# One-core attention and mixture-of-experts block: ring of 16 token tiles, weight copies two tiles ahead, last scatters in a row, loops written out

## What is computed

```python
x = x + _layernorm(_L0_attn_ref(_layernorm(x), ...))    # 16 heads of 8, relative bias, causal; MLP 128-512-128
x = x + _layernorm(_L0_ffn_ref(_layernorm(x), ...))

# _L0_ffn_ref, per token t:
probs = softmax(x @ router_w.T)            # 8 experts
top_w, top_idx = top_k(probs, 2)
h = silu(x @ gate_w[e].T) * (x @ up_w[e].T)    # 128 -> 352
y = sum over the two experts of top_w * (h @ down_w[e].T)   # 352 -> 128
```

## Time and profile before

| | us |
|---|---|
| median of 3 runs | 609.92 (609.04 to 613.66) |
| profiled execution, its own time | 612.49 |
| its span | 610.7 |

### The profile page before, as it was taken

How to read it: one execution, slowest core, us unless ns; L and a number is a source line. 1 busy time by engine, 2 the same in 40 slices (tenths; PEclk the granted TensorE clock), 3 DMA queues, 4 the chain that set the end, 5 groups by cost and what they waited for, 6 DMA issues and landing times.

```text
span 610.7 us, 13818 instructions
## 1 busy us (share of the span) xinstructions
PE 532.2 (87%) x4568; PEld 386.2 (63%) x4569; DVE 382.8 (63%) x1083; ACT 396.6 (65%) x873; POOL 329.4 (54%) x337
## 2 busy tenths in 40 slices
PE   6876899989889899799899897899778979999992
PEld 5552355656466456465556564798678879999940
DVE  6627465783994974999947767363766434555344
ACT  3357898879779788878897786355353434554415
POOL 4012535536618888438877357176437754454426
PEclk9757799999999999999999999599999999999997
DMA  8755331223214323213734612022112332222074
GB/s 199 111 140 115 110 99 57 78 76 103 67 41 126 102 68 115 77 36 123 178 109 148 145 51 49 11 60 64 37 44 66 89 89 62 59 62 61 18 275 137
DMA packets 48285, 55.85 MB, mean 91 GB/s; under 512 B 7868, under 2 KB 42559, under 8 KB 46064
## 3 DMA queue, kind: packets, MB, share of 16 engines
q1 hardware_dynamic: 43872, 46.59, 28.3%
q0 software_dynamic: 4352, 8.47, 4.2%
HBM read 37.19 MB, written 18.36 MB: 91 GB/s over the span
## 4 chain that ended last, share of the span: by engine, by line
PE 49%; DVE 23%; POOL 11%; ACT 7%; issue 7%; DMA 3%; DVEq 1%; ACTq 0%; POOLq 0%; SPq 0%
PE SC L806 13%; PE OA L816 6%; PE OA L683 5%; PE M L757 4%; PE M L721 4%; POOL slots L1591 3%; DVE SS L1218 2%; POOL RZ L1577 2%; PE SC L665 2%; DVE arena L406 2%; DVE A L1477 2%; ACT arena L927 2%; DVE STP L1287 1%; PE SC L669 1%; PE M L649 1%
## 5 line engine op out<-in xcount | busy, mean ns | idle before, releaser
L927 ACT ACTIVATE arena<-SC 128x1024 f32<-128x1024 f32 x160 | 163.0, 1033 | 20.8 <-PE SC L670 12.3
L806 PE MATMUL SC<-arena 128*128 128x128 f32 (+1 forms) x864 | 110.8, 279 | 10.9 <-DVE arena L1385 10.9
L1597 POOL DMA_INDIRECT ytok<-YSA,XGA x72 | 74.8, 1038 | 80.4 <-ACT YSA L1030 71.5
L806 PEld LDWEIGHTS SC<-arena 128*128 128x128 f32 (+1 forms) x864 | 102.5, 186 | 14.0 <-DVE arena L1385 12.8
L683 PE MATMUL OA<-arena 128*32 128x256 f32 (+1 forms) x1536 | 91.4, 357 | 10.0 <-DVE arena L1251 6.1
L1591 POOL DMA_INDIRECT slots<-XBA,IDX x64 | 74.4, 1162 | 47.6 <-DVE IDX L1336 31.1
L1024 ACT ACTIVATE arena<-SC 128x256 f32<-128x256 f32 (+1 forms) x144 | 39.2, 324 | 78.2 <-PE SC L806 78.1
L1379 DVE TENSOR_TENSOR arena<-arena,SC 128x256 f32<-128x256 f32 (+1 forms) x144 | 44.2, 348 | 70.0 <-ACT arena L1024 70.0
L683 PEld LDWEIGHTS OA<-arena 128*32 128x32 f32 x1536 | 39.4, 110 | 49.6 <-issue 19.8
L406 POOL TENSOR_TENSOR arena<-arena 128x512 f32<-128x512 f32 x32 | 41.5, 1298 | 53.8 <-ACT arena L927 53.4
L816 PE MATMUL OA<-arena 128*128 (+1 forms) x432 | 60.2, 275 | 0.7 <-DVE arena L1379 0.7
(11 more groups left out here) (216 smaller groups left out, 1002.1 us busy)
## 6 DMA issues: line engine op xcount, KB each, us to landing
arena<-parts SPq DMA_DIRECT2D x90, 192.0 KB
parts<-arena SPq DMA_DIRECT2D x16, 384.0 KB, 2.5
XGA<-slots SPq DMA_DIRECT2D x72, 65.0 KB
arena<-ytok SPq DMA_DIRECT2D x8, 512.0 KB, 6.9
X<-in_L_attn_x SPq DMA_DIRECT2D x4, 512.0 KB, 5.3
arena<-toe SPq DMA_DIRECT2D x16, 128.0 KB, 5.9
out<-X SPq DMA_DIRECT2D x8, 256.0 KB, 2.3
arena<-parts SPq DMA_DIRECT2D x12, 96.0 KB
```

What stands on the lines that cost most here:

```text
L806: mm = pe.matmul(SC[0:n, r % 2, 512 * m + P * c:512 * m + P * (c + 1)], WSEL[r % 2][:, I * m + i0:I * m + i0 + n], XGT[r % 2], start=True, ...
L927: act.activation(EB[u], SC[:, n % 2, :], ACT.Exp).then_inc(exp_done, 1)
L1597: pool.indirect_dma_start(out=ytok_d.ap(), out_offset=bass.IndirectOffsetOnAxis(ap=XG[r][:, D + 1:D + 2].bitcast(I32), axis=0), in_=YS[r], ...
```

## The change

RING becomes 16: 8 more places for XG and YS lie in the arena where the table TAB was, so the load of tile 8 waits for the last multiplications with TAB, and from tile 16 on a load waits for the result of tile s-16 in place of s-8. The weights have 4 places in place of 2, and VectorE's step s holds select(s+2) in place of select(s+1). The three hardware loops and SyncE's are written out, steps 39 and 40 included: step 39 now holds xt(40) and evac_x(40). The 16 last scatters go in positions 4 to 7 of body 9, four to a position, in place of positions 3 to 13, two to a position. The pads start at tile 32 in place of 31. In the final stage VectorE normalizes and adds batch 7 itself, before it adds batch 6, and the store of 7 goes ahead of that of 6. GpSimd's order in the final stage is the same as before.

```diff
-RING = 8
+RING = 16
+INNER = 8
-    dict(yroot=10, aroot=13, xroot=14, sc0=3, sc1=4, sc2=6, sc3=7, sc4=9, sc5=10, sc6=12, sc7=13))
+    dict(yroot=10, aroot=13, xroot=14, sc0=4, sc1=4, sc2=5, sc3=5, sc4=6, sc5=6, sc6=7, sc7=7))
-PADS_AT = 31
+PADS_AT = 32
...
+        XGB = arena[:, 8192:8192 + (RING - INNER) * ROW]
+        YSB = arena[:, 8192 + (RING - INNER) * ROW:8192 + (RING - INNER) * (ROW + D)]
-        WSEL = [arena[:, 2 * I * r:2 * I * (r + 1)] for r in range(2)]
+        WSEL = [arena[:, 2 * I * r:2 * I * (r + 1)] for r in range(4)]
...
             def load(s, r, it):
-                if not isinstance(s, int) or s >= RING:
+                if s == INNER:
+                    by_dve, by_pool = muls(NB - 1, GROUPS)
+                    sp.wait_ge(mul_dve, by_dve)
+                    sp.wait_ge(mul_pool, by_pool)
+                if s >= RING:
                     sp.wait_ge(ys_out[r], 16 * it)
...
-            with sp.Fori(EARLY // RING, STILES // RING) as it:
-                for r in range(RING):
-                    load(RING * it + r, r, it)
+            for s in range(EARLY, STILES):
+                load(s, s % RING, s // RING)
             for r in range(RING):
-                sp.wait_ge(ys_out[r], 16 * STILES // RING)
+                sp.wait_ge(ys_out[r], 16 * len(range(r, STILES, RING)))
-            for b in range(NB):
+            for b in (*range(NB - 2), NB - 1, NB - 2):
                 store(sp, b)
...
-            xt(EARLY, 0, 16 * (EARLY // RING + 1))
-            with pe.Fori(EARLY // RING, STILES // RING - 1) as it:
-                for r in range(RING):
-                    step(RING * it + r, r, it)
-            for s in range(STILES - RING, STILES + 1):
+            for s in range(EARLY, STILES + 1):
                 step(s, s % RING, s // RING)
...
-            def select(s, r):
-                dve.tensor_copy(WSEL[r % 2], WALL[:, bass.ds(weights_offset(dve, s), 2 * I)]).then_inc(wsel_rdy, 1)
+            def select(s):
+                if s in (FIRST, EARLY):
+                    dve.wait_ge(table_rdy, 2 if s == FIRST else 3)
+                dve.tensor_copy(WSEL[s % 4], WALL[:, bass.ds(weights_offset(dve, s), 2 * I)]).then_inc(wsel_rdy, 1)
             def step(s, r):
-                if not isinstance(s, int) or s + 1 not in (EARLY, STILES):
-                    select(s + 1, r + 1)
+                if s + 2 < STILES:
+                    select(s + 2)
                 hidden(s, r)
...
+            dve.wait_ge(f_rstd, NB // 2)
+            for t in range(T):
+                i = T * (NB - 1) + t
+                last = dve.tensor_scalar(FY[NB - 1][:, 0, t, :], SUMS[NB - 1][:, P * t:P * (t + 1)], MV[:, i, 0:1], RSR[:, 0, i:i + 1],
+                                         ALU.subtract, ALU.mult)
+            link(last)
+            x1 = X[:, T * (NB - 1):T * NB, :]
+            dve.tensor_tensor(x1, x1, FY[NB - 1][:, 0], ALU.add).then_inc(f_out[0], 1)
             residual(NB - 2)
-            residual(NB - 1)
```

More of the change, by code:

```diff
@@ L90, in block_kernel @@
     starts = bucket_starts(BUCKETS, 128)
-    assert (S, D, DH, T, H) == (512, P, 8, 4, 16) and STILES % RING == 0
+    assert (S, D, DH, T, H) == (512, P, 8, 4, 16)
     slots_d = nc.dram_tensor("slots", [(E * REGION + P), ROW], F32)
@@ L198, in block_kernel @@
         SCM = sb("SCM", [P, 2, max(FIRST, EARLY - FIRST, STILES - EARLY), E])
[L200 to L203, removed]
+        XGA = sb("XGA", [P, INNER * ROW])
+        YSA = sb("YSA", [P, INNER * D])
+        XGB = arena[:, 8192:8192 + (RING - INNER) * ROW]
+        YSB = arena[:, 8192 + (RING - INNER) * ROW:8192 + (RING - INNER) * (ROW + D)]
+        XG = [a[:, ROW * r:ROW * (r + 1)] for a, n in ((XGA, INNER), (XGB, RING - INNER)) for r in range(n)]
+        YS = [a[:, D * r:D * (r + 1)] for a, n in ((YSA, INNER), (YSB, RING - INNER)) for r in range(n)]
         WSX = sb("WSX", [P, 3 * 512])
@@ L298, in block_kernel @@
         out_done = [sem("out_done0"), sem("out_done1")]
-        assert EARLY % RING == 0 and EARLY * P <= 2 * (NTOK - 2 * S) - E * (P - 1)
-        assert FIRST % RING == 0 and FIRST * P <= 2 * (NTOK - 4 * S) - E * (P - 1)
+        assert EARLY * P <= 2 * (NTOK - 2 * S) - E * (P - 1)
+        assert FIRST * P <= 2 * (NTOK - 4 * S) - E * (P - 1)
         block = ctx.enter_context(nc.Block())
@@ L409, in store @@
         def store(sp, b):
-            sp.wait_ge(f_out[b % 2 if b < NB - 1 else 0], b // 2 + 1 if b < NB - 1 else NB // 2 + 1)
+            done = {NB - 2: NB // 2 + 1, NB - 1: NB // 2}.get(b, b // 2 + 1)
+            sp.wait_ge(f_out[b % 2 if b < NB - 1 else 0], done)
             sp.dma_start(out_v[:, T * b:T * (b + 1), :], X[:, T * b:T * (b + 1), :]).then_inc(out_done[b % 2], 16)
@@ L437, in weights_offset @@
         def weights_offset(eng, s):
-            at = slice(s, s + 1) if isinstance(s, int) else bass.ds(s, 1)
-            return eng.value_load(SRI[0:1, 1, at], min_val=0, max_val=(E - 1) * WEXP)
+            return eng.value_load(SRI[0:1, 1, s:s + 1], min_val=0, max_val=(E - 1) * WEXP)
         @block.sync
@@ L543, in load @@
             def load(s, r, it):
-                at = slice(s, s + 1) if isinstance(s, int) else bass.ds(s, 1)
-                row = sp.value_load(SRI[0:1, 0, at], min_val=0, max_val=DUMMY)
-                if not isinstance(s, int) or s >= RING:
+                row = sp.value_load(SRI[0:1, 0, s:s + 1], min_val=0, max_val=DUMMY)
+                if s == INNER:
[3 more added lines that the diff above has]
+                if s >= RING:
                     sp.wait_ge(ys_out[r], 16 * it)
@@ L801, in gu @@
                 pe.wait_ge(wsel_rdy, s + 1)
-                if isinstance(s, int) and s + 1 in (EARLY, STILES):
+                if s + 1 == STILES:
                     pe.wait_ge(xt_rdy, s + 1)
@@ L1032, in step @@
             def step(s, r):
-                if not isinstance(s, int) or s + 1 not in (EARLY, STILES, STILES + 1):
+                if s + 1 < STILES:
                     evac_x(s + 1, r + 1)
-                if not isinstance(s, int) or s < STILES:
+                if s < STILES:
                     silu(s, r)
-                if not isinstance(s, int) or s >= 1:
+                if s >= 1:
                     evac_y(s - 1, r - 1)
@@ L1124, in _ @@
                         step(s, s % RING)
[L1127 to L1130, removed]
-            for s in range(STILES - RING, STILES + 1):
+            for s in range(EARLY, STILES + 1):
                 step(s, s % RING)
-            for b in range(NB):
+            for b in range(NB - 1):
                 if b % 2 == 0:
@@ L1494, in _ @@
                             dve.wait_ge(table_rdy, 1)
-                            select(0, 0)
+                            select(0)
+                            select(1)
                         step(s, s % RING)
-            dve.wait_ge(table_rdy, 3)
-            select(EARLY, 0)
-            with dve.Fori(EARLY // RING, STILES // RING - 1) as it:
-                for r in range(RING):
-                    step(RING * it + r, r)
-            for s in range(STILES - RING, STILES):
+            for s in range(EARLY, STILES):
                 step(s, s % RING)
@@ L1642, in _, with residual @@
                 put(s, s % RING)
+            def residual(b):
+                pool.wait_ge(f_ln, b + 1)
+                x1 = X[:, T * b:T * (b + 1), :]
+                pool.tensor_tensor(x1, x1, FY[b][:, 0], ALU.add).then_inc(f_out[1], 1)
             for q in range(NB // 2):
```

24 lines of the change are left out of this document (10 added, 14 removed).

## The result

| | us |
|---|---|
| changed kernel, median of 20 runs | 609.37 (606.56 to 612.61) |
| kernel before, 20 runs beside them | 611.94 (608.97 to 616.13) |
| ratio | 0.9951, 95% interval 0.9933 to 0.9970 |
| profiled execution, its own time | 611.01 |

What follows compares the result with a forecast made beforehand. TensorE was taken to bound the tiles at 2.11 us each, with losses at three places and a final-stage end it doesn't set. 2.0 + 6.1 + 1.3 - 0.2 + 1.0 = 10.2 us, giving median 599.7, range 597 to 603.5.

Steps and rivals of the forecast that it cites:

- rival 2: A gives nothing or B comes back in part: 602.5, or 603.1 with D at 0.4; 17%.
- A: Tiles 13 to 23, TensorE waiting for select copies: selecting two tiles ahead gives 2.0 us.
- B: Tiles 31 to 35, TensorE waiting for token-row loads: ring of 16 and scatters in a row give 6.1 us.
- C: From tile 39 to 40, where the written-out code ended: no loop boundary gives 1.3 us.
- SyncE's waits: SyncE's final wait: eight satisfied waits follow the one ending last, a loss of 0.2 us.
- D: End of the final stage: VectorE normalizing batch 7 ends the last addition sooner and gives 1.0 us.
- The lower bound: D gives only 0.4 us if three stores closer together queue at the DMA engines.
- Rival 3: GpSimd's scatters in a row cost more; at 2.4 us an item the kernel is 1% slower (616.6); 3%.
- the rule against the change: VectorE fp32 copies lock GpSimd out of the shared port; scatters would end 47 us later, all gain gone.
- Rival 4: Written-out code of tiles 40 to 63 isn't fed fast enough; 0.43 us each takes all gain back: 610; 3%.

Runs made afterwards that it cites:

- ring16_oldsc: Changed kernel with the last scatters at their old positions 3 to 13, ring of 16 kept: 608.72 us, 0.9935 of the kernel before.
- keep_both: Changed kernel with useless matmuls in TensorE's pauses of tiles 13 to 22 and 4 more behind the last tile: 605.37 us, 0.9885 of the kernel before.
- no_ahead3: Changed kernel with the select one tile ahead again, in a set without ScalarE's stand-stills: 608.75 us, 0.9941 of the kernel before.
- pe_shift2: Changed kernel with sixteen unused one-column TensorE matmuls near the start, in a set without ScalarE's stand-stills: 606.82 us, 0.9906 of the kernel before.

## Why the prediction was wrong

The forecast span of 600.5 missed the measured 609.3 by 8.8 us. The sign was right, the time of 609.37 lies outside the range, and beyond rival 2 too.

- **A, -2.0, measured +0.5: the step that failed.** Three parts.
  - (a) 1.65 us: it was said that gu(16) keeps its distance, and its start does (2.14 behind the norm's start, 2.03 before). But the pauses moved from ahead of gu to ahead of down, and behind those of 2.33 and 0.79 us the clock was at half over gu(16) and down(15). hidden(17) comes 10.90 behind the norm in place of 9.25. With the pauses filled it is 9.49, so the clock costs 1.4 and 0.24 stays. The working followed every wait and held every duration fixed; no rival had the clock in it. That the two pauses had to come together is not shown: in ring16_oldsc the clock was at half already in down(14) (1.65 us in place of 0.93), ahead of the 0.79.
  - (b) 0.65 us: VectorE's chain from hidden(17) to hidden(21) moved up by 0.4 in place of 1.07, with the clock full too (14.54 in keep_both against 14.96). The table load moves up by 0.73, as evac_y(17) now starts 1.11 behind the end of hidden(17) and not 1.84. VectorE's small operations behind it then take 0.3 longer: the row of L1349 (L1352 before) is 0.39 us in place of 0.22. That comes with the scatters in a row, not with A. In all four traces with the scatters at their old positions it is 0.21 or 0.22, no_ahead3 without A has the 0.39, and from hidden(17) to hidden(21) ring16_oldsc takes 14.18.
  - (c) 0.2 us: from hidden(21)'s start to gu(23) 1.63 in place of 1.44.
- **B, -6.1, and C, -1.3: right.** 101.4 us from gu(23) to gu(71), as foretold. Put(22) went out at 486.1 where 481.8 was said, since the first scatter came at 459.7 and not 455.9 and the 19 items took 1.37 each without the IOTA. The scatters in a row were not needed.
- **SyncE's waits, +0.2, measured +0.35:** a wait of 0.03 has 0.03 of issue between it and the next, which the row of a single wait didn't show.
- **D, -1.0, measured 0:** the step itself is right (0.93), but the sum took the end of the last addition for the end of the span. The lower bound named the stores; they took 0.3, as SyncE's DRAIN follows the addition by 2.86 us in place of 2.54. The other 0.6 went to GpSimd's DRAIN, which no term had.
- **Not in the sum at all, +1.9 and +1.4:** the late landing of the last result, and behind it a pause of TensorE of 3.0 us, after which the first eight sums ran at half clock. The prediction counted waits on SyncE there but held the landing fixed.
- **The start, +1.9 up to the norm:** gu(0) lies between 385.0 and 389.4 us in the nine traces of kernels at 604 to 616 us whose program up to there does the same (pe_shift2 aside), 385.0 twice in changed ones. No effect of the change can be told from that spread.
- **Rival 3 and the rule against the change:** scatters and copies stood side by side and cost next to nothing more, 1.37 an item against 1.34 before. The Trainium skill, page "SBUF — State Buffer", section "A bandwidth-pool intuition that's wrong", tells of a DMA of GpSimd's queue that takes 3100 ns beside a VectorE copy in place of 620. Here the trace agrees in direction only: between 455 and 492 us a GpSimd DMA row that overlapped a select copy by over 0.3 us took 1.16 us on average, the others 1.00, and in the kernel before 1.14 and 0.99. Rival 4 fell too: every written-out tile from 23 to 71 came at 2.11.

## What to carry to other kernels

Moving a wait on TensorE isn't free even where nothing behind it waits longer: look at the granted clock over the work behind each pause, and fill the pauses with matmuls if it falls. Measure an edit at the end to the end of the span, not to the last computation, and look at the closing row of every engine's queue. And a transfer that everything waits for can meet an instruction packet of another engine; where code grows or moves, look at its landing time again.

## What the runs showed of the hardware

- An instruction packet of 16 KB takes 0.9 to 1.4 us, and where it began 1.3 to 1.6 us behind the issue of an indirect DMA, two small packets of that DMA ended just behind it: landing 3.3 to 3.95 us in place of 2.09. Sixteen matmuls of one column on TensorE, 550 us earlier in the program, took that away.
- TensorE fell to 1.2 GHz at gu(16) in all nine traces with two tiles ahead whose pauses were left open, and in none of the four with filled pauses. With one tile ahead it fell over gu(15), behind a pause of 2.3 us, in three traces of the slow sets and not in the two others. So one pause of 2.3 us was followed by either clock; what decides is open.
- It was at 1.2 GHz in the first sums behind pauses of 2.5 to 3.1 us, in ten traces: sixteen pieces took 8.7 to 8.8 us. With pauses of 1.4 us or less, or none, they took 7.0 to 7.5, in eight.
- GpSimd's closing DRAIN took 6.45 us and ended the changed kernel's span, 0.6 us behind SyncE's. What it waits for is open.
- Two of four sets ran every kernel 4% slower, with ScalarE at rest for about 4 us at a time and nothing in the profile to release it. None of the kernels with open pauses beat the kernel before there. The cause is open.
